# Weighing a chunk in two halves of its queries, with a pair of scores and two tiles of maxima ahead of each half

## The reference

```python
# layer 0, sparse: keys of a query = strided keys (every 8th) + its own block of 128
w = jnp.einsum('bhnqd,bhnkd->bhnqk', fq, fk) * scale + fmask
w = jax.nn.softmax(w, axis=-1)
o1 = jnp.einsum('bhnqk,bhnkd->bhnqd', w, fv)
# layer 1, twice (rotary heads; normed heads)
scores = jnp.einsum('bhqd,bhkd->bhqk', Q, K) / math.sqrt(Dh)
scores = jnp.where(causal, scores, jnp.finfo(scores.dtype).min)
attn = jax.nn.softmax(scores, axis=-1)
y = jnp.einsum('bhqk,bhkd->bhqd', attn, V)
```

## Time and profile before

| | |
|---|---|
| median of 3 runs | 5375.74 us (5335.63 to 5381.57) |
| the profiled execution | 5351.09 us, its span 5349.2 us |
| granted TensorE clock, mean | 0.916 |
| PE busy | 4794.5 us (90%) |
| DVE busy | 4064.9 us (76%) |
| ACT busy | 2852.4 us (53%) |
| POOL busy | 284.4 us (5%) |
| matmuls, weight loads | 31872 each |

### The profile page before, as it was taken

How to read it: one execution, slowest core, us unless ns; L and a number is a source line. 1 busy time by engine, 2 the same in 40 slices (tenths; PEclk the granted TensorE clock), 3 DMA queues, 4 the chain that set the end, 5 groups by cost and what they waited for, 6 DMA issues and landing times.

```text
span 5349.2 us, 82616 instructions
## 1 busy us (share of the span) xinstructions
PE 4794.5 (90%) x31872; PEld 2551.8 (48%) x31872; DVE 4064.9 (76%) x9211; ACT 2852.4 (53%) x3317; POOL 284.4 (5%) x339
## 2 busy tenths in 40 slices
PE   5377989676599999999999999999999999899999
PEld 4244445566244333443334443333443333588888
DVE  7465757577488898889998888998889977455555
ACT  3234545322155666666676666677566777432322
POOL 2010000133000000000000000000000000300000
PEclk8778989887578999999999999999999999899999
DMA  4633221355600030030120210200300000201010
GB/s 151 172 72 66 43 53 27 111 189 192 125 17 13 7 52 12 21 54 9 15 38 15 40 32 9 37 16 23 59 10 5 9 9 10 69 21 40 21 40 9
DMA packets 226730, 255.84 MB, mean 48 GB/s; under 512 B 69329, under 2 KB 170705, under 8 KB 224017
## 3 DMA queue, kind: packets, MB, share of 16 engines
q1 hardware_dynamic: 216512, 190.12, 12.5%
q0 software_dynamic: 9824, 60.43, 7.0%
HBM read 143.99 MB, written 104.92 MB: 47 GB/s over the span
## 4 chain that ended last, share of the span: by engine, by line
PE 70%; DVE 19%; issue 5%; DMA 4%; ACT 2%; SPq 1%; POOL 0%; DVEq 0%; ACTq 0%; POOLq 0%
PE psum L782 22%; PE psum L713 19%; PE psum L76 13%; DVE maxes_dense L862 11%; PE psum L741 4%; PE psum L679 3%; PE psum L702 2%; DMA queries_sparse<-neg_rows_sparse 1%; PE psum L723 1%; PE psum L750 1%; PE psum L1541 1%; DVE masked_scores_dense L855 1%; DMA x_in<-in_L_attn_hidden_states 1%; DMA keys_sparse<-parts_scratch 1%; PE psum L709 1%
## 5 line engine op out<-in xcount | busy, mean ns | idle before, releaser
L819 ACT ACTIVATE probs_dense<-psum 128x1024 f32<-128x1024 f32 (+3 forms) x2304 | 2068.4, 950 | 996.7 <-PE psum L741 746.7
L862 DVE TENSOR_REDUCE maxes_dense<-psum 128x1 f32<-128x512 f32 x3584 | 2227.8, 683 | 227.3 <-PE psum L713 226.2
L713 PE MATMUL psum<-keys_dense,queries_dense 48*128 48x512 f32 (+3 forms) x4608 | 1553.6, 477 | 138.1 <-DMA queries_dense<-parts_scratch 54.8
L713 PEld LDWEIGHTS psum<-keys_dense,queries_dense 48*128 48x128 f32 x4608 | 667.5, 191 | 1490.8 <-DVE maxes_dense L862 1142.1
L782 PE MATMUL psum<-probs_dense,values_dense 128*32 128x512 f32 (+3 forms) x9216 | 1176.6, 588 | 0.0
L741 PE MATMUL psum<-queries_dense,keys_dense 50*128 50x512 f32 (+3 forms) x4608 | 809.3, 407 | 11.8 <-ACT probs_dense L819 11.5
L855 DVE CUSTOM_DVE_ANT_0 masked_scores_dense<-psum,causal_add 128x128 f32<-128x128 f32 (+3 forms) x1024 | 452.2, 488 | 175.6 <-PE psum L713 156.0
L741 PEld LDWEIGHTS psum<-queries_dense,keys_dense 50*128 50x128 f32 x4608 | 448.6, 193 | 106.8 <-ACT probs_dense L819 60.8
L855 DVE CUSTOM_DVE_ANT_0 masked_scores_sparse<-psum,after_add 128x512 f32<-128x512 f32 x512 | 326.4, 688 | 173.2 <-PE psum L702 172.2
L1648 ACT ACTIVATE activated<-psum 128x512 f32<-128x512 f32 x208 | 124.7, 599 | 414.1 <-PE psum L76 401.6
L819 ACT ACTIVATE probs_sparse<-psum 128x1024 f32<-128x1024 f32 x224 | 217.6, 1022 | 207.3 <-PE psum L679 78.9
(11 more groups left out here) (297 smaller groups left out, 5379.9 us busy)
## 6 DMA issues: line engine op xcount, KB each, us to landing
v_scratch<-ve_s SPq DMA_DIRECT2D x96, 256.0 KB, 2.7
parts_scratch<-part_high SPq DMA_DIRECT2D x24, 1024.0 KB, 4.2
parts_scratch<-part_low SPq DMA_DIRECT2D x24, 1024.0 KB, 6.7
queries_dense<-parts_scratch SPq DMA_DIRECT2D x384, 64.0 KB
keys_dense<-parts_scratch POOLq DMA_DIRECT2D x42, 512.0 KB, 17.7
values_dense<-v_scratch POOLq DMA_DIRECT2D x8, 2048.0 KB, 34.5
queries_sparse<-parts_scratch SPq DMA_DIRECT2D x192, 64.0 KB
keys_sparse<-parts_scratch POOLq DMA_DIRECT2D x18, 512.0 KB, 17.6
```

The lines of the kernel that those rows point to most:

```text
L713: m = pe.matmul(bank[:, 0:width], q[rows(h, TROWS), h // 2, b * P:(b + 1) * P], k[rows(h, TROWS), h // 2, kc * STRIP:kc * STRIP + width], ...
L819: act.activation(probs[i % 6][:, :, first_col:STRIP], psum[:, at2:at2 + 2, first_col:STRIP], ACT.Exp, scale=SCALE, **extra).then_inc(exp_d ...
L862: m = dve.tensor_reduce(mx[:, h * BLOCKS + b, kc:kc + 1], bank, AX.X, ALU.max)
```

## The change

The weighing of a chunk becomes two steps, one for queries 0 to 255 and one for queries 256 to 511, and the list is written in another order: first a pair of scores, two tiles, the first half of the chunk before; then the other pair, two tiles, the second half. The tiles that stood ahead of a chunk's scores now stand behind its first pair. The first chunk of a unit (c = 0) is weighed whole, in its second half, since its first matmul into the bank also clears it. In diagonal chunks the first half is cut to the columns that exist; where none exist (the last two diagonal chunks) that half has no matmuls. In the local chunk of the sparse stage each half has two of the four blocks of queries. `weighed` is counted up by the second half alone. Code behind the hunk lies 1 to 6 lines further down (L782 is L787 in the changed kernel, L862 is L868).

```diff
@@ -526,16 +527,16 @@
             order.append(("unit", n, None))
             for c in range(sizes[n]):
                 m = ends[n] - sizes[n] + c
-                emit_tiles(4 * (m + lead(n)) + 2)
-                for h in range(GROUP):
-                    order.append(("score", n, (m, c, h)))
-                    if n >= 1 and c == 1 and h == 3:
+                for half in range(2):
+                    order.append(("score", n, (m, c, 2 * half)))
+                    order.append(("score", n, (m, c, 2 * half + 1)))
+                    if n >= 1 and c == 1 and half == 1:
                         order.append(("out", n - 1, None))
-                    if h % 2 == 1:
-                        emit_tiles(4 * (m + lead(n)) + (2, 4)[h // 2])
-                if c >= 1:
-                    order.append(("weigh", n, (m - 1, c - 1)))
-            order.append(("weigh", n, (m, c)))
+                    emit_tiles(4 * (m + lead(n)) + 2 * half + 2)
+                    if c >= 1:
+                        order.append(("weigh", n, (m - 1, c - 1, half)))
+            order.append(("weigh", n, (m, c, 0)))
+            order.append(("weigh", n, (m, c, 1)))
         order.append(("out", len(units) - 1, None))
 
 
@@ -761,8 +762,8 @@
                                                   start=False, stop=(b == BLOCKS - 1))
                         m.then_inc(scored, 1)
                     else:
-                        m_at, c = what
-                        if c == 0:
+                        m_at, c, half = what
+                        if c == 0 and half == 1:
                             pe.wait_ge(values_in[n // STRIPS % 2], 16 * (n // STRIPS // 2 + 1))
...
@@ -770,19 +771,24 @@
                         pe.wait_ge(exp_done, 2 * m_at + 2)
                         local = sparse and c == NSTR // P
-                        for b in (range(BLOCKS) if local else (None,)):
+                        first_col = max(half * STRIP // 2 if c else 0, 0 if sparse else (c - BLOCKS * j) * P)
+                        last_col = (half + 1) * STRIP // 2 if c else half * STRIP
+                        if first_col >= last_col:
+                            continue
+                        for b in (range(first_col // P, last_col // P) if local else (None,)):
                             for h in range(GROUP):
                                 own_rows = slice(h * GCOL, (h + 1) * GCOL)
                                 if local:
                                     cols, vt = slice(b * P, (b + 1) * P), v[:, BLOCKS * j + b, own_rows]
                                 elif sparse:
-                                    cols, vt = slice(0, STRIP), str_values[n // STRIPS % 2][:, c, own_rows]
+                                    cols, vt = slice(first_col, last_col), str_values[n // STRIPS % 2][:, c, own_rows]
                                 else:
-                                    cols, vt = slice(max(0, c - BLOCKS * j) * P, STRIP), v[:, c, own_rows]
+                                    cols, vt = slice(first_col, last_col), v[:, c, own_rows]
...
-                        m.then_inc(weighed, 1)
+                        if half == 1:
+                            m.then_inc(weighed, 1)
```

## The result

The changed kernel is slower: 5480.3 us median of four runs (5454.4 to 5525.0) against 5364.3 (5335.6 to 5381.6), ratio 1.023 with a 95% interval of 1.015 to 1.031. The forecast was 5300, with a range of 5215 to 5390. Every ratio here compares a kernel with the kernel before as it ran beside it, and leaves out runs over 1.5% above the fastest of the same kernel, so it can differ a little from the quotient of two medians. The profiled execution took 5478.1 us with a span of 5476.2, 127.0 us more than the one before.

What follows compares the result with a forecast made beforehand. An ordinary dense chunk was taken as bound by a 2.69 us loop between PE and DVE. Terms -104 (ordinary), +15 (diagonal), +13 (sparse) sum to -76: 5351.1 to 5275, carried to the median as 5300 us, range 5215 to 5390.

Steps and rivals of the forecast that it cites:

- W': Half a weighing on PE, four matmuls over 256 columns: forecast at 0.57 us, two halves 1.14 for 0.99 whole.
- -104 and 0: Dense stage: 550 full-width ordinary chunks at -0.19 us give -104 us; chunks with masked tiles 0, at most 10 either way.
- A tile pair that waits for nothing gives PE to W after 0.42 - 0.18 = 0.24: PE in an ordinary chunk: two unhindered tiles, their load now hidden, take 0.24 us before the weighing.
- PE has slack against DVE's 2.40: Ordinary chunk: PE without waits needs 2.30 us after, 2.05 before, both under DVE's floor of 2.40.
- the loop: Ordinary chunk: DVE reduction, late tile, weighing, next first tile wait on each other; 2.69 us before, 2.51 forecast after.
- 0.20 for 0.14 a chunk: Alternative PE price of halving the weighing: eight added matmuls at 60 cycles; total about -43 us instead of -75.
- 2.30 + 0.31 = 2.61, under 2.69: 0: Diagonal chunks with full tiles, 44 units: PE's new path plus mask matmuls stays under the old period, so no cost.
- One ordinary chunk -0.19, two chunks with masks: Sparse unit of five chunks: -0.19, twice +0.24, and +0.1 at its end; 32 x 0.4 = +13 us.
- Rival 4: More switches and openly shown loads draw the lower clock more often; 190 us more cancels the gain: 5400 us, chance 0.07.
- Rival 2: Instructions arrive too slowly, as a chunk's records rise from 32 to 48: 5508 us at 58 ns each, chance 0.12.
- Rival 3: The first half's weighing waits for ACT's exponential; waits of 0.1 to 0.2 eat the gain: 5375 us, chance 0.08.
- Rival 1: DVE reaches its 2.40 us floor in ordinary chunks, 550 x 0.30 = -165: 5226 us, chance 0.13.

## Why the prediction was wrong

**Ordinary chunks: right in size, half right in cause.** 2.51 for 2.51, W' 0.57 for 0.57. Over the chunks that ran at full clock in both kernels, full-width ones went from 2.74 to 2.58 in the mean (552 of them, -88 us), those with masked tiles cost +2 together. So -86 where -104 and 0 stood. The step "A tile pair that waits for nothing gives PE to W after 0.42 - 0.18 = 0.24" failed (0.35), so "PE has slack against DVE's 2.40" did too: PE without waits is 2.51 a chunk, not 2.30. It cost nothing there, since the loop gave the same; it cost wherever PE had been reckoned to have 0.2 us in hand. The loop itself held where it ruled, in the new order with the whole weighing. One figure of the working beside it was off: with 0.20 for 0.14 a chunk, W' would be 0.60, not 0.63. The forecast did not use it.

**The diagonal: mis-sized.** +15 was forecast, +38 came (the sum over the chunks at full clock in both). "2.30 + 0.31 = 2.61, under 2.69: 0" is the step: with PE at 2.51 the mask matmuls make 2.82. About 18 of the 38 lie in diagonal chunks with narrow tiles, near the 15 forecast; 20 lie in those with full ones, where 0 stood. The last diagonal chunk with full tiles went from 2.53 to 2.88, the third from 2.46 to 2.61.

**A place that was passed over: a unit's start.** The first two chunks were left out as having little or no weighing. At full clock they break even (the first 0.9 us shorter, the second 0.9 longer); what they do to the clock is below.

**Sparse: the step that failed most.** +13 was forecast, +111 came. "One ordinary chunk -0.19, two chunks with masks" gave +0.4 a unit; it is +1.2. The ordinary chunk, the fourth, gained nothing (2.71 and 2.71): its wait for DVE fell from 0.53 to 0.18, the rest went into PE's own longer way through it, and a wait of 0.41 came in the chunk behind it. The two chunks with masks cost +0.73 and +0.44 where +0.24 each had been taken, and the last weighing +0.34 where +0.1 had. Of the +0.73 two halves are 0.14; the rest is that two pairs of local tiles and two pairs of scores, which took 2.85 us together (740.16 to 743.01), take 3.44 when a weighing stands between them; with the whole weighing behind both, the chunk came to +0.21 alone. 32 x 1.2 = 38 us. The rest is the lower level: 181 us more of it, in which a unit takes 30.3 us against 18.8, so 181 x (1 - 18.8 / 30.3) = 69 by estimate; the forecast had no term for it in this stage. Sum 107, of 111 measured.

**Lower clock in the dense stage: "0".** 146 us more at the lower level, at 4.32 a chunk against 2.51, are 146 x (1 - 2.51 / 4.32) = +61 by estimate. With -86, +38 and -3 for the unit starts the stage comes to +10; it was +14. Rival 4 named the mechanism and mis-sized it ("190 us more would cancel everything": it was 327 in both stages), and its chance of 0.07 rested on the argument that PE does the same work in less time. That does not bear on it. What the runs show is where the time at the lower level comes from: a fall at a unit's start in every kernel, and a longer stay if the chunks behind it, and the diagonal or the first two as well, have the new order.

**The other rivals.** Rival 2 (instructions too slow) fell: 48 records in 2.51 us, 52 ns each, with no stall. Rival 3 fell: W' waits 0.24 for issue, not for ACT, in ordinary chunks. Rival 1 did not occur, since PE itself stands at 2.51. Of what was named as proof of rival 4, "the clock of the stage is under 0.93", the dense stage (0.93) just missed it; the sparse one (0.78) showed it best, and no such line had been drawn there.

**What stays open.** Why the new order in the third to sixth chunk holds the clock down only when an end of the unit has it too: with old ends, new ordinary chunks from the third on have 256 us at the lower level, no more than with the old order there. No run separates how much of the sparse stage's 181 us has the same cause. And why blocks of local tiles and scores take 0.59 us longer with a weighing between them was not taken apart.

The best version is the new order in ordinary chunks of the dense stage only: 5297 us, 0.9% under the kernel before by the ratio and about 3% under the changed one; from the seventh chunk on it is as good (5296.8).

## What to carry to other kernels

A reordering that breaks one wait pays only where the engine that was waiting has time in hand: read that stage by stage and by kind of chunk from windows at full clock, and change those chunks alone. The busy share does not tell this: it read 97% in a dense chunk that could lose 0.19 us and 98% in a sparse unit that lost nothing, so compare the starts of the engine's blocks, chunk by chunk, and look where a wait goes when it is moved. And where the clock falls at regular places, price a new order at those places too: by the estimates above, what was lost and won at full clock (38 and 51 us) nearly cancels, and about the whole loss of 127 us is time at the lower level (61 + 69), and in the right chunks alone the same change gains 0.9% (0.6 to 1.2).

## What the runs showed of the hardware that was not expected

**The clock stayed at its lower level under an engine without a gap**: 41.0 us at 0.50 with PE busy 41.00, and 15 stretches of over 12 us at that level in the dense stage after, against 7 before. The Trainium skill's page "TensorE: Matmul & The Clock Gate", Part 1, says that activity releases the throttle. This trace shows PE busy by its records all through such a stretch, so by that reading it disagrees; what of a record counts as activity, no run here tells.

**Order, not the number of instructions, moves the clock.** Splitting the weighing in the old order left the dense stage with 290 us at the lower level (291 before), at the same count of records as the changed kernel's 437; the five executions with the dense stage's order untouched or only its pieces split had 256 to 311.

**A pair of tiles costs PE as much as a pair of scores** in this order, 0.35 and 0.34 us, although its loads are hidden behind the scores.
